# Wider zero-column fillers in six slots of the ODE turns with messages, and fillers of 192 zero columns behind their four events

## What is computed

```python
def _mlp(y, W1, b1, W2, b2, W3, b3):
    h = jnp.tanh(y @ W1.T + b1)
    h = jnp.tanh(h @ W2.T + b2)
    return h @ W3.T + b3
...
    k1 = f(y)
    k2 = f(y + dt / 2 * k1)
    k3 = f(y + dt / 2 * k2)
    k4 = f(y + dt * k3)
    return y + dt * (k1 + 2 * k2 + 2 * k3 + k4) / 6
```

## Time and profile before

| | us |
|---|---|
| median of 3 runs | 7550.15 |
| lowest, highest | 7517.82, 7563.33 |
| the profiled execution | 7540.8 |
| its span | 7539.2 |
| mean granted clock of the span | 0.91 |

### The profile page before, as it was taken

The page is one execution under the profiler, slowest core; times in us unless marked ns, Lnnn a source line. Parts: engine busy times, 40 slices in busy tenths (PEclk is TensorE's granted clock), DMA queues, the critical chain, the costliest instruction groups (busy, mean ns, idle before and its releaser), DMA issues. The chain is left out here.

```text
span 7539.2 us, 491413 instructions
## 1 busy us (share of the span) xinstructions
PE 6262.1 (83%) x209707; PEld 4152.9 (55%) x209707; DVE 2608.7 (35%) x12046; ACT 1697.6 (23%) x8390; POOL 891.6 (12%) x2042
## 2 busy tenths in 40 slices
PE   6857989999999999999778998899889987888741
PEld 5524555555555555555466776677667765666520
DVE  5323444444444422111123332333323332222257
ACT  0122333333333333333201111111111111111111
POOL 0011111111111168300000000000000000000000
PEclk9967888889888899999889999999999999999975
DMA  1021111111111111000032221122112221111100
GB/s 45 0 51 29 28 28 28 29 28 29 28 28 28 29 39 43 14 0 0 14 117 39 40 40 26 29 43 40 31 24 41 43 36 7 7 7 7 20 13 7
DMA packets 814823, 213.43 MB, mean 28 GB/s; under 512 B 706441, under 2 KB 772653, under 8 KB 814724
## 3 DMA queue, kind: packets, MB, share of 16 engines
q1 hardware_dynamic: 765700, 152.75, 10.6%
q0 software_dynamic: 47872, 54.13, 2.6%
q10 hardware_dynamic: 1152, 5.15, 0.2%
HBM read 183.50 MB, written 28.16 MB: 28 GB/s over the span
## 5 line engine op out<-in xcount | busy, mean ns | idle before, releaser
L1751 PE MATMUL ps_rows<-whh,h_pair 128*4 128x320 f16 x34944 | 1323.6, 302 | 104.1 <-issue 20.5
L1073 PE MATMUL ode_busy<-ode_busy_x,ode_busy_w 128*32 128x384 f16 (+2 forms) x17216 | 1143.9, 333 | 23.7 <-issue 15.4
L1751 PEld LDWEIGHTS ps_rows<-whh,h_pair 128*4 128x4 f16 x34944 | 743.3, 84 | 538.1 <-DVE h_pair L1608 155.8
L1067 PEld LDWEIGHTS ode_psa<-ode_a,ode_w2t 128*32 128x32 f32 x19968 | 477.6, 116 | 769.6 <-ACT ode_a L1176 568.7
L1186 DVE SCALAR_TENSOR_TENSOR ode_part<-ode_b 128x1 f32<-128x1 f32 x624 | 114.0, 183 | 1902.8 <-ACT ode_b L1178 1856.4
L1620 DVE COPY gate_rows<-ps_rows_last 128x192 f32<-128x192 f32 x624 | 223.1, 358 | 1560.0 <-PE ps_rows_last L1751 1560.0
L1084 PE MATMUL ode_pso<-whh 125*32 125x170 f32 (+3 forms) x9600 | 666.4, 349 | 24.2 <-issue 23.5
L1067 PE MATMUL ode_psa<-ode_a,ode_w2t 128*32 128x1 f32 x19968 | 623.9, 184 | 51.6 <-ACT ode_a L1170 43.5
L1178 ACT ACTIVATE ode_b<-ode_psa 128x1 f32<-128x1 f32 x2496 | 427.2, 171 | 1023.5 <-PE ode_psa L1067 1021.6
L1672 ACT COPY gate_rows<-ps_rows 128x320 f32<-128x320 f32 x624 | 265.3, 425 | 1720.4 <-PE ps_rows L1751 1720.4
L1751 PE MATMUL ps_rows_last<-whh,h_pair 128*4 128x192 f16 x19968 | 526.7, 247 | 3.0 <-issue 3.0
(11 more groups left out here) (499 smaller groups left out, 9907.6 us busy)
## 6 DMA issues: line engine op xcount, KB each, us to landing
late_w<-in_wih_t SPq DMA_DIRECT2D x386, 128.0 KB, 2.1
xg_buf<-xg_scratch SPq DMA_DIRECT2D x1248, 16.0 KB, 2.0
split_raw<-in_whh_t SPq DMA_DIRECT2D x64, 256.0 KB, 2.6
ig_w<-in_wih_t SPq DMA_DIRECT2D x8, 2048.0 KB, 11.9
xg_scratch<-late_out SPq DMA_DIRECT2D x24, 624.0 KB, 3.2
whh<-h_scratch SPq DMA_DIRECT2D x105, 62.5 KB, 2.3
xg_scratch<-ig_out ACTq DMA_DIRECT2D x8, 628.0 KB, 7.9
h_scratch<-mlp_h SPq DMA_DIRECT2D x40, 125.0 KB, 2.3
```

The lines of the kernel that those rows point to most:

```text
L1067: m = nc.tensor.matmul(ps[32 * j:32 * j + 32, 0:1], w[:, 32 * j:32 * j + 32], col, start=start, stop=stop, skip_group_check=True)
L1073: nc.tensor.matmul(ps_busy[32 * j:32 * j + 32, 0:cols], busy_w[:, 32 * j:32 * j + 32], busy_x[:, 0:cols], start=True, stop=True, skip_grou ...
L1751: m = nc.tensor.matmul(out[32 * j:32 * j + 4, :], hpair[:, c, 2 - 2 * part:6 - 2 * part], whh[:, at + lo:at + hi], start=(part == 0 and c ...
```

## The change

`MORE` columns are added to the filler of the six zero slots, in turns with messages only: 384 becomes 448, 320 becomes 384, in both rounds. Behind each of the four events stands a filler of one round of 192 columns.

```diff
         BUSY, BUSY_A, BUSY_B = 2, 384, 320
+        MORE, EVENT_GAP = 64, 192
...
             elif 18 <= n < 21:
                 weight_piece(0, n - 18)
             else:
-                busy(cols)
+                busy(cols + MORE)
...
             if (r, s) == (0, 1):
                 pe.wait_ge(M["vec"], i * UT + 2)
                 pe.sem_inc(M["ready"], 1)
+                busy(EVENT_GAP, 1)
             elif (r, s) == (2, 1):
                 pe.wait_ge(M["vec"], i * UT + (UT + 1))
                 pe.sem_inc(M["ready"], 1)
+                busy(EVENT_GAP, 1)
             elif (r, s) == (2, 2):
                 pe.wait_ge(M["h3_in"], i * 16 + 32)
                 pe.sem_inc(M["ready"], 1)
+                busy(EVENT_GAP, 1)
             elif (r, s) == (3, 2):
                 pe.wait_ge(M["added"], i + 2)
                 pe.sem_inc(M["ready"], 1)
+                busy(EVENT_GAP, 1)
             else:
                 busy(BANK, 1)
```

## The result

| | before | changed |
|---|---|---|
| median, us | 7546.91 (4 runs, 7517.82 to 7563.33) | 7411.53 (4 runs, 7410.51 to 7420.07) |
| ratio, 95% interval | | 0.9819 (0.9803 to 0.9835) |
| the profiled execution, its span | 7540.8, 7539.2 | 7420.07, 7418.4 |
| turns with messages (100) | 2059.8 | 1940.8 |
| turns without (56) | 985.4 | 987.7 |

The change made the kernel 135 us faster, outside the range that was forecast. By the two profiled executions the spans differ by 120.8 us, and 119.0 of them lie in the turns with messages.

What follows compares the result with a forecast made beforehand. It took ScalarE's chain, the gathers' stalls and the low clock to bound the message turns. From 7540.8 us, 62 won on the clock and 12 lost on wider slots gave -50, so 7491 us, range 7430 to 7560.

Steps and rivals of the forecast that it cites:

- The two losses: Message turns: time beyond 17.1 us of stages goes to GpSimd's gathers twice a turn and to the low clock, 155 us.
- What it gives: Stretches around the gathers: added 0.09 to 0.36 us against 0.54 to 0.67 missing wins 40% of 155, 62 us.
- The slots ahead of the gathers: Up to three wider slots ahead of a gather add 0.06 us each to the thin stretch.
- Slots at half clock: Six wider slots aren't hidden at half clock, 0.12 us each: 12 us with 40% fewer falls, 20 us otherwise.
- rival 3: Wider slots and event fillers hold the next quarters, 0.72 us a turn, no fall avoided: 7613 us; chance 0.08.
- the cover of the event fillers: Four fillers of 192 columns behind the events are hidden, cost 0; uncovered 36 us.
- Rival 1: Message turns: the clock falls stay, since 0.09 us at an event is small; 7551 us, chance 0.17.
- the rule of the Trainium skill: Clock is lost only when TensorE idles longer than these rows show; gaps of 0.57 and 0.70 us cost none.
- Rival 2: Message turns: nearly all clock falls go, 130 us off, 7411 us, PEclk 0.97; chance 0.09.
- That nothing else moves: The 56 turns without messages stay about 985 us; ScalarE, VectorE, GpSimd and SyncE keep their rows.

Runs made afterwards that it cites:

- the stalls by hand: Kernel before, with ScalarE copying zeros that nothing reads at two places of each message turn: 7546.96 us, against 7236.82 for the kernel before in that job.

## Why the prediction was wrong

*The two losses.* Right, and they can now be priced apart. A turn is 17.5 us with neither stall nor low clock (1754.0 / 100), 19.05 with the gathers' stalls at full clock, 20.6 with both. So the stalls cost some 150 us by themselves, and the clock the 155 that the prediction took; the change touches the second alone. The run with the stalls by hand shows that the second follows from the first.

*What it gives: this is the step that failed.* "I take 40% of the loss: 0.4 x 155 = 62 us." The profiled execution won 119 of 155 us, 77%; of the 594 us at 1.2 GHz 130 were left. The 40% came from setting what the change adds (0.09 to 0.36 us) against what two stretches missed beside the thinnest that kept its clock (0.54 and 0.67), and from taking that share of the hole for the same share of the falls. Four things in it don't hold.

- The measure of the hole. 3.13 us was the thinnest of the few stretches that had been read. In the same trace, inside the very turns that the earlier trace rows shows at full clock, a stretch with a gather kept its clock at 2.59 us busy, as thin as those before the falls:

```profile
1826.30:1829.70 3.40, 2.59 (x111) 1.63 (x111) 1.20 (x6) 0.99 (x6) 1.41 (x2) 1.00 0.00 0
1829.70:1833.10 3.40, 3.28 (x139) 1.83 (x142) 0.53 (x4) 1.22 (x8) 0.00 (x0) 1.00 0.26 71
```

- The size of the addition. 0.09 us is a price of columns, the hole is busy time of rows, and there the filler's row is 0.27 us. The upper end is a slip besides: 0.09 and three times 0.06 make 0.27, not 0.36.
- Busy time as the currency. One column behind each event has a row of 0.19 us, more than the 0.09 that was counted for 192, and wins 15 us, not clear of noise; 192 columns have one of 0.27 and win 141 us (both with the stalls by hand).
- The share. 0.09 us were 13% and 17% of the holes, and the event fillers won most of the loss.

What a stretch must hold to keep the clock isn't shown by these runs, so why these columns end some three falls of four stays open.

*The slots ahead of the gathers.* The prediction counted them as up to 0.18 us of the gain. With stalls by hand they won 16 us by themselves, not clear of noise and with as many falls, and nothing beside the event fillers (7406.02 with both, 7405.49 without the slots). The events' fillers did the work: the first 53 us, the second and third 88.

*Slots at half clock: 12 us.* Measured: none visible. 113 of the 130 us of half-rate time that are left lie behind the first gather, where the next slots carry messages and nothing is wider; where the clock is at 1.00 the six slots cost nothing (1.0000, 0.9990 to 1.0010). That they are hidden at full clock was right, and so rival 3 falls. So was the cover of the event fillers: 192 columns are hidden, while 512 cost 11 to 12 us, so the cover ends between these widths.

*Rival 1* (the falls stay) and the rule of the Trainium skill, "TensorE: Matmul & The Clock Gate", beside it, which foretold the same: shown wrong for this kernel. The clock is lost behind hand-made idle times of 0.90 us as well, and the change won it back. *Rival 2* (nearly all falls go, 7411) had a chance of 0.09 and came nearest: its clock, 0.97, is the measured one, and 87 of 122 falls went. That its time is within 1 us of the median is luck: it took 130 us off, and the profiled executions differ by 121. Its reason, that the gather then meets the chain at the same place each time, no run tested. What I held against it, that no filler stands in the slots beside and right behind the gather, was no obstacle: the fillers behind the events were enough.

*That nothing else moves:* right; 985.4 and 987.7 us for the turns without messages.

## What to carry to other kernels

Where the granted clock is low in a stage, find the stretches before each fall and what is thin in them; a filler right behind the stall (here 192 columns in four matmuls), where the chain waits anyway, can win back the clock, and costs nothing as long as the next work isn't held by it. Don't price it by busy time: read all the stretches that kept the clock, not a few, and measure one column against many. Try each group of places alone: with the stalls by hand the four event fillers won everything, and the six wider slots beside them nothing (7406.02 against 7405.49). And the stall that opens the hole may be there in some runs and not in others: compare with the kernel before in the same job, and price the stall itself, since here its absence was worth 314 us (7547 against 7233) and the fillers 135.

## What the runs showed of the hardware that was not expected

- GpSimd's gather of 125 rows, 1.22 us by its own row in every trace with gathers, goes with a stall of TensorE and ScalarE in some jobs and not in others, with the same program: ScalarE idles 1.08 and 1.26 us instead of 0.36, and the kernel before takes 7547 to 7554 us with the stalls and 7232 to 7237 without, 4%. In the earlier trace rows and in the changed kernel TensorE stops inside a group of eight matmuls, waiting for nothing that the profile shows, and goes on within 0.1 us of the gather's end (2013.27 behind 2013.19, 1432.05 behind 1432.01). What decides whether it happens isn't known from these runs; the same chip showed both.
- With TensorE idle for 0.57 and 0.70 us at the two gathers of a turn, among fillers that otherwise hold 2.4 GHz, the clock fell to 1.2 GHz 122 times in 100 turns; with stalls by hand (0.90 us at one of them) 166 times. With four matmuls of 192 zero columns behind each event these were 35 and 42 times, and with four matmuls of one column 165.
